# Turning the softmax probabilities by a DMA transpose in place of TensorE transposes

## The reference

```
x = x + L0(x)    # attention; weights also scaled by a coherence term, a field term added
x = x + L1(x)    # masked attention, RMS norm of its output, scale and shift
x = x + L2(x)    # h = norm(x); x + attention(h); then x + swiglu(norm(x)), hidden 2048
x = x + L3(x)    # mix of the quarters

q, k, v = x @ Wq.T, x @ Wk.T, x @ Wv.T          # (b, h, i, d)
p = softmax(q @ k^T / sqrt(32))                  # (b, h, i, j), 128 x 128 per head
out = p @ v                                      # contraction over j
```

## Time and profile before

| | us |
|---|---|
| median of 2 runs (3266.89 to 3268.45) | 3267.67 |
| span of the profiled execution | 3266.8 |
| TensorE busy in it | 3106.6 (95%) |
| VectorE, ScalarE, GpSimd busy | 2031.8, 1369.6, 614.0 |

### The profile page before, as it was taken

The page is one execution under the profiler, slowest core; times in us unless marked ns, Lnnn a source line. Parts: engine busy times, 40 slices in busy tenths (PEclk is TensorE's granted clock), DMA queues, the critical chain, the costliest instruction groups (busy, mean ns, idle before and its releaser), DMA issues. The chain is left out here.

```text
span 3266.8 us, 64344 instructions
## 1 busy us (share of the span) xinstructions
PE 3106.6 (95%) x24853; PEld 2688.4 (82%) x24853; DVE 2031.8 (62%) x3739; ACT 1369.6 (42%) x2123; POOL 614.0 (19%) x340
## 2 busy tenths in 40 slices
PE   6999999998899999994999999959999999999998
PEld 5989898997788888884888989848888888888886
DVE  5666666665577777775777777755544445556544
ACT  3444444443555555553555555532222223222221
POOL 2112211220122222211111121112222221111111
PEclk8999999999999999997999999979999999999999
DMA  4221222121322222223222222241122232111111
GB/s 153 47 64 51 56 53 64 51 52 48 102 65 64 64 64 64 65 52 110 65 64 71 71 64 71 59 142 52 52 65 72 69 104 73 44 52 39 51 39 39
DMA packets 198918, 216.27 MB, mean 66 GB/s; under 512 B 17537, under 2 KB 173313, under 8 KB 198305
## 3 DMA queue, kind: packets, MB, share of 16 engines
q1 hardware_dynamic: 198816, 214.87, 22.7%
HBM read 122.53 MB, written 41.94 MB: 50 GB/s over the span
## 5 line engine op out<-in xcount | busy, mean ns | idle before, releaser
L783 ACT ACTIVATE L_pth<-L_bank_t 128x512 f16<-128x512 f32 x384 | 227.7, 593 | 380.5 <-PE L_bank_t L614 380.5
L787 ACT ACTIVATE L_shifted<-L_shifted,keep_lift 128x512 f32<-128x512 f32 x384 | 277.2, 722 | 236.6 <-DVE L_shifted L942 234.1
L1516 DVE TENSOR_TENSOR mlp_act_t<-mlp_bank_u,mlp_sg 128x512 f32<-128x512 f32 x128 | 88.5, 691 | 453.3 <-ACT mlp_sg L1418 449.6
L938 DVE TENSOR_REDUCE L_top<-L_bank_s 128x4 f32<-128x512 f32 x384 | 263.1, 685 | 129.5 <-PE L_bank_s L563 65.1
L1418 ACT ACTIVATE mlp_sg<-mlp_bank_g 128x512 f32<-128x512 f32 x128 | 76.6, 598 | 628.6 <-PE mlp_bank_u L1331 628.5
L1558 POOL TENSOR_TENSOR mlp_al<-mlp_act_t,mlp_ah 128x512 fp32r<-128x512 f32 x128 | 175.0, 1367 | 856.3 <-ACT mlp_ah L1424 856.3
L946 DVE TENSOR_TENSOR L_ptl<-L_bank_t,L_pth 128x512 f16<-128x512 f32 x384 | 262.7, 684 | 63.9 <-ACT L_pth L783 60.6
L1121 POOL TENSOR_TENSOR L_vr<-L_vf,keep_v 128x1024 f32<-128x1024 f32 x48 | 99.2, 2067 | 1045.6 <-ACT keep_v L817 1045.6
L630 PEld LDWEIGHTS L_bank_o<-keep_v,L_pth 128*128 128x128 f16 x4608 | 199.0, 96 | 97.6 <-issue 72.6
L942 DVE TENSOR_TENSOR L_shifted<-L_bank_s,L_top 128x512 f32<-128x512 f32 x384 | 265.5, 691 | 16.7
L561 PE MATMUL L_bank_a<-L_xh,L_wkh 128*128 128x256 f32 x768 | 233.7, 304 | 37.7 <-DVE L_wkl L101 24.6
(11 more groups left out here) (272 smaller groups left out, 8925.8 us busy)
## 6 DMA issues: line engine op xcount, KB each, us to landing
keep_kbh<-L_kh SPq DMA_DIRECT2D x384, 64.0 KB, 2.1
keep_kbl<-L_kl SPq DMA_DIRECT2D x384, 64.0 KB, 2.1
resid<-L_xres SPq DMA_DIRECT2D x48, 512.0 KB, 2.6
L_xf<-resid SPq DMA_DIRECT2D x32, 512.0 KB, 3.7
L_xres<-resid SPq DMA_DIRECT2D x32, 512.0 KB, 3.3
mlp_xf<-resid SPq DMA_DIRECT2D x32, 512.0 KB, 4.5
mlp_res<-resid SPq DMA_DIRECT2D x32, 512.0 KB, 4.6
L_xf<-in_x SPq DMA_DIRECT2D x16, 512.0 KB, 3.3
```

The costliest lines, as they stand in the source:

```text
L783: nc.scalar.activation(pth[:, u % 2], bank_t[u % 2][:].rearrange("p (h j) -> p h j", h=4), ACT.Copy).then_inc(p_high, 1)
L787: nc.scalar.activation(shifted[:, u % 2], shifted[:, u % 2], ACT.Exp, bias=k["lift"][:, 0:1], scale=SCALE).then_inc(exp_done, 1)
L938: nc.vector.reduce_max(top[:, u % 2, :], src, AX_X).then_inc(top_ready, 1)
```

## The change

Per unit, the exponentials are no longer turned on TensorE. ScalarE copies `shifted` to float16 in `pq[.., 0]`, VectorE writes the remainder to `pq[.., 1]`, both in SBUF, and SP issues one DMA transpose of the 128 x 1024 float16 tile `pq[u % 2]` into `pt[u % 4]`, from where `weigh_values` takes its weights. What moves with it:

- `shift_scores` waits for its own engine's `low_probs` of two units earlier instead of the turn; `high_probs(u)` follows `exponentials(u)` in the same slot, and waits until the DMA of unit u - 2 has landed.
- `value_slot(u)` becomes min(u + 4, 10). `normalise` goes from slots 4, 6, 8, 9 to 5, 7, 9, 10; in L0 `add_field` from 6 and 9 to 7 and 10; `turn_output(i, 1)` and the split of its result from slot 10 to 11; `first_values` from 10 to 11; in L2 `squares` from slot 2 to 4.
- Slot 0 no longer begins with a piece of the output projection: `scores(0)` is the first matmul (in L0 behind `coherence`), and both pieces follow.
- SP issues the eight turns of a group in order, and the loads, stores and four parts of `spread_keys` between them.
- The columns of `v2` and `v3` go from 34 to 32. `ident_r` and `mask` become bf16, so the mask matmul of L1 is bf16. Two PSUM banks are free, and SBUF holds more.

```diff
-        pth, ptl = sb("pth", [P, 2, 4, P], F16), sb("ptl", [P, 2, 4, P], F16)
+        pq = sb("pq", [P, 2, 2, 4, P], F16)
+        pt = sb("pt", [P, TURNED, 2, 4, P], F16)
...
-            return min(u + 3, UNITS + 1)
+            return min(u + 4, 10)
...
+            def turn_probs(i, u):
+                n = UNITS * i + u
+                if positive(n - TURNED + 1):
+                    sp.wait_ge(pv_done, n - TURNED + 1)
+                    sp.sem_inc(turn_free, 1)
+                sp.wait_ge(p_low, n + 1)
+                sp.sem_inc(turn_begun, 1)
+                sp.dma_start_transpose(pt[:, u % TURNED].rearrange("p n h j -> p (n h) j"),
+                                       pq[:, u % 2].rearrange("p n h j -> p (n h j)")).then_inc(pt_ready[u % TURNED], 16)
+
             def body(i):
...
+                for u in range(UNITS):
+                    turn_probs(i, u)
+                    if u == 1 and L1 and positive(i):
+                        load_residual(i - 1)
+                    if u == 1 and not L1 and positive(i):
+                        store(i - 1)
+                    if u == 0 and has(i, 2):
+                        load(i + 2)
+                    if u == 4 and not L1:
+                        load_residual(i)
+                    if has(i, 1):
+                        for part in {5: (0,), 6: (1, 2), 7: (3,)}.get(u, ()):
+                            spread_keys(i + 1, part)
+                if L1 and positive(i):
                     store(i - 1)
...
-            def turn_probs(i, u):
-                n = UNITS * i + u
-                pe.wait_ge(exp_done, n + 1)
-                if positive(n - 1):
-                    pe.wait_ge(p_low, n - 1)
-                for h in range(4):
-                    mm = nc.tensor.transpose(bank_t[u % 2][:, h * P:(h + 1) * P], shifted[:, u % 2, h, :], k["ident"][:])
-                mm.then_inc(t_full, 1)
...
-                pe.wait_ge(p_low, n + 1)
+                pe.wait_ge(pt_ready[u % TURNED], 16 * (UNITS // TURNED * i + u // TURNED + 1))
...
-                    ahead = 1 if s in (0, UNITS, UNITS + 1, UNITS + 2) else 0
+                    ahead = 1 if s in (UNITS, UNITS + 1, UNITS + 2) else 0
...
-                    if s == 10:
+                    if s == 11:
                         turn_output(i, 1)
...
-                act.wait_ge(t_full, n + 1)
+                act.wait_ge(exp_done, n + 1)
                 if positive(n - 1):
-                    act.wait_ge(pv_done, n - 1)
-                nc.scalar.activation(pth[:, u % 2], bank_t[u % 2][:].rearrange("p (h j) -> p h j", h=4), ACT.Copy).then_inc(p_high, 1)
+                    act.wait_ge(pt_ready[(u - 2) % TURNED], 16 * (UNITS // TURNED * i + (u - 2) // TURNED + 1))
+                nc.scalar.activation(pq[:, u % 2, 0], shifted[:, u % 2], ACT.Copy).then_inc(p_high, 1)
...
-                nc.vector.tensor_tensor(ptl[:, u % 2], bank_t[u % 2][:].rearrange("p (h j) -> p h j", h=4), pth[:, u % 2], ALU.subtract).then_inc(p_low, 1)
+                nc.vector.tensor_tensor(pq[:, u % 2, 1], shifted[:, u % 2], pq[:, u % 2, 0], ALU.subtract).then_inc(p_low, 1)
...
-                    if s in (4, 6, 8, 9):
-                        normalise(i, (4, 6, 8, 9).index(s))
+                    if s in (5, 7, 9, 10):
+                        normalise(i, (5, 7, 9, 10).index(s))
```

More of the change, by code:

```diff
@@ L28 @@
 VW = HD + 2
+TURNED = 4
 T = 256
@@ L173, in _ @@
                 nc.gpsimd.memset(f32(t[:]), 0.0)
-            for t in (k["v1"], k["v2"], k["v3"]):
-                nc.gpsimd.memset(t[:], 1.0 if t is k["v1"] else 0.0)
+            nc.gpsimd.memset(k["v1"][:], 1.0)
         @block.tensor
@@ L418, in attention @@
         s_full, top_ready, shift_done, exp_done = sem("s_full"), sem("top_ready"), sem("shift_done"), sem("exp_done")
-        t_full, p_high, p_low = sem("t_full"), sem("p_high"), sem("p_low")
+        p_high, p_low = sem("p_high"), sem("p_low")
+        pt_ready = [sem(f"pt_ready{n}") for n in range(TURNED)]
+        turn_free, turn_begun = sem("turn_free"), sem("turn_begun")
         pv_done, rz_step, o_free = sem("pv_done"), sem("rz_step"), sem("o_free")
@@ L520, in spread_keys @@
                     sp.wait_ge(a_free[m], a_done(p, ("k", m)))
[L521 to L524 removed]
+                dst, src = ((kbh, kh), (kbl, kl))[low]
+                for h in range(4):
+                    rows = slice(HD * h, HD * (h + 1))
+                    sp.dma_start(f32(dst[b][rows, :, h, :]), f32(src[rows, :, b * P:(b + 1) * P])).then_inc(kb_ready[b], 16)
             load(0)
@@ L530, in _ @@
                 ws.load(sp, n)
-            spread_keys(0, 0)
-            spread_keys(0, 1)
+            for part in range(4):
+                spread_keys(0, part)
             sp.wait_ge(ws.low_done, len(ws.loads))
@@ L624, in weigh_values @@
                         pe.wait_ge(o_free, o_turn(i, u // 2))
-                pe.wait_ge(p_low, n + 1)
+                pe.wait_ge(pt_ready[u % TURNED], 16 * (UNITS // TURNED * i + u // TURNED + 1))
                 for h in range(4):
                     o = ((u % 2) * 4 + h) * VW
-                    passes = [(p, v) for p, parts in ((pth, (v1, v2, v3)), (ptl, (v1, v2))) for v in parts]
-                    for n, (p, v) in enumerate(passes):
-                        mm = nc.tensor.matmul(bank_o[:, o:o + VW], p[:, u % 2, h, :], v[:, b, 4 * c + h, :], start=(n == 0), stop=(n == len(passes) - 1))
+                    passes = [(part, v) for part, values in ((0, (v1, v2, v3)), (1, (v1, v2))) for v in values]
+                    for m, (part, v) in enumerate(passes):
+                        mm = nc.tensor.matmul(bank_o[:, o:o + (VW if v is v1 else HD)], pt[:, u % TURNED, part, h, :], v[:, b, 4 * c + h, :],
+                                              start=(m == 0), stop=(m == len(passes) - 1))
                 mm.then_inc(pv_done, 1)
@@ L701, in body @@
                             weigh_values(i, u)
[L702 to L706, removed]
                     project_pieces(pieces[s][ahead:])
@@ L859, in body @@
                         high_output(i, 0)
-                    if 1 < s <= UNITS or (s == 1 and L0):
-                        high_probs(i, s - 1)
                     if s < UNITS:
                         exponentials(i, s)
-                    if s == 1 and not L0:
-                        high_probs(i, 0)
+                        high_probs(i, s)
                     if s == 0:
                         second_values(i)
-                    if s == 2 and L2 and has(i, 2):
+                    if s == 4 and L2 and has(i, 2):
                         act.wait_ge(x_loaded, 16 * (i + 3))
@@ L879, in body @@
                             read_fill(group_of(i, fill), fill)
-                    if s == 10 and has(i, 1):
+                    if s == 11 and has(i, 1):
                         first_values(i + 1)
@@ L1582, in build @@
         k["ones"] = keep("ones", [P, P])
-        k["ident_r"], k["mask"] = (keep(n, [P, P], F32R) for n in ("ident_r", "mask"))
+        k["ident_r"], k["mask"] = (keep(n, [P, P], BF16) for n in ("ident_r", "mask"))
         k["ones_b"] = keep("ones_b", [P, P], BF16)
```

29 lines of the change are left out of this document (10 added, 19 removed).

## The result

The changed kernel takes 3553.2 us (median of two runs, 3553.1 to 3553.3) against 3267.7 before: 1.087 times as long, 95% interval 1.084 to 1.090. The forecast was 3204, so 349 us are to be explained: the 64 that did not come and 286 that were lost.

A forecast was written before the change was run, and what follows sets the result against it. TensorE, busy 95%, was taken as the bound, a group lasting as long as its list of work. Terms -140 + 42 + 7 + 17 + 10 = -64 us took 3267.7 to 3204 us; range 3135 to 3315.

The forecast's parts named there:

- third, who waits: DMA waiters: `weigh_values(u)` three slots later, and ScalarE's `high_probs(u)` for unit u - 2, with `exponentials(u + 1)` and VectorE's next work behind.
- L is free up to about 3.3 us: Landing time L, taken as 3.0 us, costs nothing up to there: VectorE's loop between subtractions has 3.4 us plus 0.8 other work.
- second rival: Wait for the DMA takes the turn's place (landing around 4.5 us): +81 us in L1 and L2, 3285 us; chance 0.19.
- Behind SP's wait are queued the loads, stores and spread keys; I count 0 for them: SP's queue behind its wait for `p_low`: those issues are due slots later, so 0 us.
- third rival: SP's queue becomes the bound, eight turns a group issued one by one: 3460 us at 3 us held per issue; chance 0.19.
- TensorE's saving: Transposes leave TensorE: 0.39 us a unit, 3.1 us a group, -140 us over 45 groups.
- the mask at no change: Mask matmul in bf16 keeps its 512 columns: taken as 0, up to -10 us for the range.
- the wait before the first scores: Group start, `scores(0)` first: TensorE stalls 1.6 us for the query split, 1.4 net, 15 group changes of L1 and L2: +42 us.
- forecast +7: Group start in L0, coherence matmuls still in between: 0.45 us stall, 15 times.
- ScalarE's copy: Float16 copy now reads SBUF: 722 ns against 593, +0.13 us a unit, hidden by ScalarE's idle share.
- the +17 at the end of a group: TensorE waits for the fourth `normalise` before the second `turn_output`: 0.8 us in L1, 0.3 in L2, 15 times.
- forecast as +10: Last groups, where only the DMA chain runs: 3 us a layer and a little drain.

The follow-up runs named there:

- e5: Changed kernel with a thin transpose: the DMA turns only one 128x128 block of the eight, the rest stay at ones; 3426.6 us, 1.049.
- e3: Changed kernel with the x load (from the third group on) and residual load bringing 32 of 256 columns, the rest stale; 3481.1 us, 1.065.
- e9: Changed kernel with ScalarE's copies of finished projection halves (key split) ahead of `high_probs` in slots 0 to 7; 3379.3 us, 1.035.
- e1: Changed kernel with four float16 probability buffers instead of two in L1 and L2, so `high_probs(u)` waits for u - 4; 3442.2 us, 1.053.
- f2: Changed kernel with only the order moves of e9, e10, e12 and e4; its buffers, bank and loads as they are; 3263.8 us, 0.999.
- e12: e10 plus e9's move, with the first `turn_output` behind slot 8's value products and its VectorE split behind the last subtraction; 3202.2 us, 0.981.
- f1: Changed kernel with only the last transpose of a group issued ahead of key copies 2 and 3; 3523.6 us, 1.079.
- e10: e1 plus e4, second output bank, later first `turn_output`, L2 squares behind key split, early x load, last transpose ahead of key copies 2 and 3; 3306.2 us, 1.012.
- e4: Changed kernel with one piece of the output projection ahead of the first scores again; 3513.1 us, 1.075.
- e2: Changed kernel with two PSUM banks of outputs in turn instead of one; 3599.2 us, 1.101.

## Why the prediction was wrong

The step that failed is "third, who waits", with its conclusion "L is free up to about 3.3 us".

1. **The operation was judged well.** Landing: 2.8 us alone, taken as 3.0. Hold of SyncE: 1.25 us, taken as 1.5. The Trainium skill's figure (VectorE: DVE Perf Modes, The three transpose paths), eight times over 10.5 us, does not carry over: one block took 2.2 us (e5), eight in one call 2.8; nor were the 0.7 us reached that the prediction estimated from the Trainium skill (Advanced Engine Details and Errata, X-Bar Transpose).
2. **It was taken as one number.** Two transposes of eight, in L2 three, have a load or a store at their side, which the new SyncE loop puts there, and land in 3.6 to 5.3 us. The step tested 3.0 against 3.3 for every unit. This is the second rival's case, and its sign and its signature (ScalarE's wait for the DMA) are what came. But 3.3 was no safe line either: in e3 the landings lie under it in the median of every place, and 277 of the 349 us are still there. The step's loop counts 0.8 us of other work on VectorE between two subtractions; in the first slots of the L1 group there is none.
3. **The wait was priced at its own length.** The step named the waiter, `high_probs`, and behind it only the next exponential. Also behind it in program order was the key split, and behind VectorE's half of that the shift and `normalise`. The second rival allowed 81 us for a chain through VectorE's softmax work alone. What the runs showed in place of "free": e9 leaves the wait nearly unchanged in sum (204 us for 218), and 174 us go by taking the split out from behind it. e1 is the other half: take the wait away in L1 and L2 and leave the order, and 111 us go. The moves of order together give back 289 (f2).
4. **The clock.** Behind the 3.90 us of idle time at 1019.04 TensorE runs at half its speed, 1.2 instead of 2.4 GHz, here in stretches of 2 us:

```profile
1013.00:1015.00 2.00, 2.00 (x15) 1.53 (x13) 0.00 (x0) 0.12 (x1) 0.00 (x0) 1.00 1.03 217
...
1018.00:1020.00 2.00, 0.96 (x22) 0.97 (x23) 1.83 (x6) 1.35 (x2) 0.00 (x0) 0.78 0.00 0
1020.00:1022.00 2.00, 2.00 (x11) 2.00 (x11) 1.97 (x4) 0.72 (x1) 0.00 (x0) 0.50 0.58 131
```

   TensorE is busy 46.43, 38.34 and 37.22 us in a group and 43.11, 37.13 and 35.24 in e12, with the same instructions, within three, at clock 1.00. That is 6.5 us x 16 = 104 us. The pages of the whole program, with 23317 matmuls in either run, give 3065.7 - 2974.9 = 91 us, a quarter of the gap:

```profile
PE 2974.9 (93%) x23317; PEld 2535.6 (79%) x23317; DVE 2085.9 (65%) x3739; ACT 1380.2 (43%) x2123; POOL 619.8 (19%) x338
```

   e9 has 3007.2 us, so some 59 of its 174 us are time that TensorE itself no longer loses at the low clock. Both are estimates, since the ends of busy time are modelled. The prediction priced no stall by what the clock adds.
5. **"Behind SP's wait are queued the loads, stores and spread keys; I count 0 for them"** looked at what stands behind the transposes, not at how the transposes stand behind the copies: 30 us alone (f1), 63 once the rest was short (e10). The third rival had this queue, but as a sum over a group; the place was one transpose behind 5.2 us of issues.
6. **Right:** TensorE's saving (2.9 us a group by e12's windows, forecast 3.1, in busy time whose ends are modelled); the mask at no change:

```profile
L623 PE MATMUL L_bank_s<-keep_mask,keep_ident_r 128*128 128x512 bf16 x128 | 51.9, 406 | 0.0
```

   and the wait before the first scores, forecast as 1.6 us 30 times in L1 and L2: 48.0 us, 30 times, 1.6 the longest. Its worth was not the sum's, as e4 shows by layer. L0 has none of it (forecast +7). The sum's own terms make the L1 group 39.87 - 3.1 + 1.4 + 0.8 = 39.0 us, and not the 38.6 that the prediction names. ScalarE's copy costs less than feared, 631 ns rather than 722, against 593 before.
7. **Wrong place:** the +17 at the end of a group. No idle time stands before the second `turn_output` in the L1 group; it stands before the first (1.09 us). Its `normalise` had moved from slot 6 to 7 as well, and I followed only the third and fourth. The idle time before the first `turn_output` is 38, 14 and 18 us in the first 15 groups of L0, L1 and L2. The last groups with what follows them, forecast as +10, took 22 us more than in the kernel before, and 12 more in e12.

With the chains cut, the groups of e12 are 44.2, 39.1 and 36.5 us, the forecast's 43.9, 38.6 and 36.7, and its time 3202 against 3204. That is partly chance: e12 has no wait for the query split, which the forecast had at 42 us, and has others, and it has the buffers, the bank and the early load, which the forecast kernel had not. Still, TensorE's busy time supports the sum of work (131.7 us less than before over the program, forecast 140); what was missing was the order in which the engines meet it. Why the second bank turns from a loss to a gain is not shown beyond the merged waits and the lower clock of e2. What the kernel before would gain from such moves was not tried; TensorE idles for 0.02 to 0.25 us in its groups.

## What to carry to other kernels

When a step gets a longer or more variable latency, list everything that stands behind the wait in program order on that engine, follow each item to the bottleneck engine, and only then ask how long the wait is: moving an unrelated step in front of it was worth as much as making the buffers deeper where both could be done, and it needed no memory. Price a DMA by its landing beside the transfers that will run with it, and look at what the queue must issue ahead of it. The largest wait on the bottleneck engine can be the shadow of another: relieving it first made the kernel slower, relieving it last made it faster.

## What the runs showed of the hardware

- A transposing DMA of 256 KB held SyncE for 1.25 us, twice a key copy's 0.64, and landed in 2.8 us; beside a load of 512 KB it took 4.1 and 5.3 in the L1 group shown. A store of 512 KB near both loads and transposes landed in 4.2 us (median), instead of 2.6 before the change, 2.9 with thin loads (e3) and 2.8 with thin transposes (e5).
- VectorE's subtraction with both operands in SBUF was slowed while GpSimd worked: 684 ns in the mean before, when one operand was in a bank, 769 after. Of the 384 subtractions after, the 331 with no GpSimd work beside them take at most 0.69 us, the 47 that have it for over half a microsecond 0.97 to 1.85. GpSimd is busy with L1116 and L1127 from 1001.53 to 1006.51; the two subtractions in that time take 1.01 and 1.19 us, and the maximum and the shift between them, which read a bank, their usual 0.69:

```profile
1003.49 1.01 DVE L948 TENSOR_TENSOR L_pq<-L_shifted,L_pq 128x512 f16<-128x512 f32 x1
1004.53 0.69 DVE L940 TENSOR_REDUCE L_top<-L_bank_s 128x4 f32<-128x512 f32 x1
1005.25 0.69 DVE L944 TENSOR_TENSOR L_shifted<-L_bank_s,L_top 128x512 f32<-128x512 f32 x1
1005.86 1.19 DVE L948 TENSOR_TENSOR L_pq<-L_shifted,L_pq 128x512 f16<-128x512 f32 x1
```
